# A graph-network kernel on one core: a block's table rows stored by one transfer of 125 rows in place of 112 and 13

## The chip, the core and the metric

The kernel runs on one core of one Trainium2 chip. The metric is device microseconds of one execution. Times and clocks of engines below are from the hardware profiler; PE is TensorE, DVE is VectorE, ACT is ScalarE, POOL is GpSimd, SP is SyncE.

## What is computed

`x` is 6250 nodes by 256 features, f32. After a layer norm it goes through three relational graph layers, a linear-attention mixer and a mixture of 8 experts. The change lies in the graph layers:

```python
def _rgcn_layer(x, W, root, bias, src, dst, seg):
    agg = jax.ops.segment_sum(x[src], seg, num_segments=N_REL * N_NODES)
    agg = agg.reshape(N_REL, N_NODES, -1)
    return jnp.einsum('rnd,rde->ne', agg, W) + x @ root + bias
...
for l in range(N_LAYERS - 1):
    h = jax.nn.relu(_rgcn_layer(h, weights[l], roots[l], biases[l], src, dst, seg))
h = jax.nn.sigmoid(_rgcn_layer(h, weights[-1], roots[-1], biases[-1], src, dst, seg))
```

There are 206,250 edges, sorted by `dst`, and 8 relations. Products and sums commute, so the kernel multiplies first: for each layer it makes a table in HBM that holds, for each node, its features times each of the 8 relation matrices (8 rows of 256 f32 a node, 8 KB), and then each edge fetches one 1 KB row of that table and adds it to its destination.

## The kernel before

Nodes are cut into NW = 50 blocks ("windows") of WIN = 125 nodes, one node a partition. Internally the stages are phase 0 (layer norm and the table of layer 1) and phases 1 to 3, one for each graph layer; in this text they are the first stage and layers 1, 2, 3. Each of layers 1 and 2 also makes the table of the next layer, block by block, behind its own sums, and layer 1 carries the mixer's projections, layer 2 its attention and MLP, layer 3 the experts.

POOL issues the gathers (L501): 1612 indirect transfers a layer, each of 128 edges (128 KB), into a ring of 8 chunks of 4 gathers in SBUF. Before a chunk it waits on `slots_free`, which PE raises; before a layer it waits (L486) until all stores of that layer's table have landed. SP turns landed gathers into `chunks_ready` (L428). DVE builds one-hot matrices (L994), and PE adds a block's gathered rows into PSUM with them (L1403). About 32 gathers fall to a block.

The table of the next layer: PE transposes the block's result (L1343), ACT copies it to `hT` (L564), PE multiplies it with the weights (`products`, L1371), and the results leave PSUM for `y_stage[parity]`, one of two buffers of 125 partitions: relation pairs 0, 2, 3 by ACT and pair 1 by DVE (`evac_y`, L517 and L835). Before it writes, `evac_y` waits on `table_stored[parity]`: the store of two blocks earlier has to have landed. Then `store_y` (L520) issues the block's stores from ACT's queue: 112 and then 13 partitions of 8 KB each, and in layers 1 and 2 a third, 125 partitions of 1 KB to `base`. Each transfer raises its semaphore by 16 in all. The last block of a stage or layer is stored by another function, `evac_and_store` (L533), in pieces of 4, 2 and 2 relations.

All transfers but SP's early loads and POOL's gathers go through ACT's queue, between ACT's own arithmetic and in program order. What is issued around the store:

- First stage, for each block: the table store of the block before, then the store of normalized rows to `xn_scratch` (L595, 125 x 1 KB), the load of `x` four blocks ahead (L597, 125 x 1 KB), the copy to `hT` (L564), and the next `evac_y`. Early in this stage SP loads the edge arrays, weights and vectors; among these `dst` twice for an order check (L384: 125 partitions of 6,600 B; L385: 124 of them).
- Layer 1: table store, `base` store, the load of the next block's `xn_in` (L627), then `xhat` (L630).
- Layer 2: table store (L527), `base` store (L530), `res_scratch` store (L740), loads of `base_in` (L619), `xn_in` (L699), `x_in` (L700), each 125 x 1 KB; only behind these seven issues stands the ACTIVATE of `xhatT` (L724) in ACT's program. PE needs `xhatT` for the MLP's up-projection (L1558), which stands between the third and fourth of the units of L1403 in PE's program (`phase2`).
- Layer 3 stores no table.

Of the kernel before, what the change touches and what calls it, by code (L numbers as in the profile page):

```python
# [26 lines left out]
WIN = 125  # L27
WIN_A = 112
# [8 lines left out]
def gps_program(nc, t):  # L37
    nodes, D = t["x"].shape
    edges = t["src"].shape[0]
    R = t["L0_gnn_weights"].shape[1]  # L40
    ROWS = R + 1
    K = D // 128
    NW = nodes // WIN
# [24 lines left out]
    table_nodes = [a.rearrange("(n r) d -> n (r d)", r=R) for a in table]  # L68
# [4 lines left out]
    with ExitStack() as ctx:  # L73
        ctx.enter_context(nc.allow_non_contiguous_dma(reason="a few vectors go to a feature a partition"))

        def sb(name, shape, dt=FP32):
            return ctx.enter_context(nc.sbuf_tensor(name, shape, dt))

        def sem(name):
            return ctx.enter_context(nc.semaphore(name))  # L80
# [18 lines left out]
        y_stage = [sb(f"y_stage{i}", [WIN, ROWS * D]) for i in range(2)]  # L99
# [146 lines left out]
        table_stored = [sem(f"table_stored{i}") for i in range(2)]  # L246
# [64 lines left out]

        def stored_before(phase, turn, parity=0):

            whole = 32 if phase == 0 else 48
            earlier = (32 + 48 * (phase - 1)) * (NW // 2) if phase else 0
            return earlier + turn * whole + (4 * 16 * phase if parity else 0)

        S_CHAIN, P2_CHAIN, P3_CHAIN, R_CHAIN = 3, 15, 13, 9

# [20 lines left out]
        def dve_blocks_before(phase, w):  # L340

            return w if phase == 0 else NW + ((phase - 1) * NW + w) * 2
# [94 lines left out]
        def _(pool):  # L437
# [45 lines left out]
            for l in range(3):  # L483

                for i in range(2):
                    pool.wait_ge(table_stored[i], stored_before(l + 1, 0, i))  # L486
                with pool.Fori(0, passes) as p:
                    before = pool.snap((passes * l + p) * CHUNKS)
                    for chunk in range(CHUNKS):
                        s = chunk % RING  # L490

                        if chunk >= CHUNKS - RING + LAST_CHUNKS:
                            continue
                        pool.wait_ge(slots_free, before + (chunk + 1))
                        apart(pool)
                        for j in range(TILES):
                            c = s * TILES + j
                            tile = chunk * TILES + j
                            n = min(TILE, edges - tile * TILE)
                            assert n > 0  # L500
                            nc.gpsimd.indirect_dma_start(  # L501
                                ring[0:n, c * D:(c + 1) * D], None, table[l],
                                bass.IndirectOffsetOnAxis(ap=gather_idx[0:n, tile:tile + 1].bitcast(U32), axis=0)
                                ).then_inc(gathered[s], 16)
# [3 lines left out]
        def _(act):  # L508
            def evac_y(phase, win, blocks):

                w, parity, turn = win
                T = w + phase * NW
                if 0 in blocks and not (phase == 0 and isinstance(w, int) and w < 2):
                    act.wait_ge(table_stored[parity], stored_before(phase, turn, parity))
                for b in blocks:
                    act.wait_ge(y_done, products_before(phase, w) + (ORDERS[phase].index(b) + 1))
                    nc.scalar.copy(y_stage[parity][:, b * 2 * D:(b + 1) * 2 * D],  # L517
                                   BANK[phase][b][0:WIN, 0:2 * D]).then_inc(y_evac_act, 1)

            def store_y(phase, win):  # L520

                w, parity, _ = win
                T = w + phase * NW
                act.wait_ge(y_evac_act, T * 3 + 3)
                act.wait_ge(y_evac_dve, dve_blocks_before(phase, w + 1))
                for p0, p1 in ((0, WIN_A), (WIN_A, WIN)):
                    act.dma_start(table_nodes[phase][bass.ds(w * WIN + p0, p1 - p0), :],  # L527
                                  y_stage[parity][p0:p1, 0:R * D]).then_inc(table_stored[parity], 16)
                if phase:
                    act.dma_start(rows(base_dram[phase - 1], w), y_stage[parity][:, R * D:ROWS * D]  # L530
                                  ).then_inc(table_stored[parity], 16)
# [35 lines left out]
            def rows(a, w):  # L567
                return a[bass.ds(w * WIN, WIN), :]
# [33 lines left out]
            def phase0_tail(win):  # L602
                evac_y(0, win, (0, 2, 3))
                store_y(0, win)
# [5 lines left out]
            for i in range(2):  # L610
                act.wait_ge(table_stored[i], stored_before(1, 0, i))
                act.wait_ge(xn_stored[i], 16 * (NW // 2))
# [8 lines left out]
            def phase1(cur, prev):  # L621
                w, parity, turn = cur
                if not (isinstance(w, int) and w == NW - 1):

                    if prev:
                        act.wait_ge(xhat_ready, w)
                    act.dma_start(xn_in[1 - parity][:, :], rows(xn_dram, w + 1)).then_inc(xn_loaded[1 - parity], 16)  # L627
                act.wait_ge(xn_loaded[parity], turn * 16 + 16)

                nc.scalar.activation(xhat[:, :], xn_in[parity][:, :], ACT.Identity,  # L630
                                     scale=ln1_scale[:, bass.ds(w, 1)],
                                     bias=ln1_shift[:, bass.ds(w, 1)]).then_inc(xhat_ready, 1)
                if prev:
                    copy_hT(1, prev, ACT.Relu)
                act.wait_ge(mixT_done, w + 1)
                for k in range(K):
                    last = nc.scalar.activation(xhatT[:, k, :], ps_a[:, k * WIN:(k + 1) * WIN], ACT.Identity,
                                                scale=cols[:, 0, k:k + 1], bias=cols[:, 1, k:k + 1])
                last.then_inc(xhatT_ready, 1)
                nc.scalar.copy(xnT[:, :, :], ps_a[:, K * WIN:2 * K * WIN].rearrange("p (k n) -> p k n", k=K)  # L640
                               ).then_inc(xnT_ready, 1)
                if prev:
                    evac_y(1, prev, (0,))
                if w < NW - 1:
                    projections(w)
                if prev:
                    evac_y(1, prev, (2, 3))
                    store_y(1, prev)
# [45 lines left out]
            def phase2(cur, prev):  # L694
                w, parity, turn = cur
                if w == 0:
                    warm(ACT.Gelu)
                load_base(1, w, parity)
                act.dma_start(xn_in[parity][:, :], rows(xn_dram, w)).then_inc(xn_loaded[parity], 16)  # L699
                act.dma_start(x_in[parity][:, :], rows(t["x"], w)).then_inc(x_loaded[parity], 16)  # L700
                if prev:
                    xhat_transposed(prev)
                    copy_hT(2, prev, ACT.Relu)
                    if w < NW - 1:
                        gelus(prev)
                    evac_y(2, prev, (0,))
                if w < NW - 1:
                    take_q(w)
                    copy_q(w + 1)
                if prev:  # L710
                    evac_y(2, prev, (2, 3))
                    store_y(2, prev)
                if prev and w < NW - 1:
                    store_res(prev)
# [1034 lines left out]
```

## Time and profile before

| | |
|---|---|
| runs | 7882.57 and 7892.93 us, median 7887.75 us |
| profiled execution, span from first to last instruction | 6522.0 us |
| profiled execution's own time | not given by the page; only the span is |
| mean granted TensorE clock | 0.920 |
| instructions | 82,564 |
| PE busy | 5410.7 us (83%) |
| POOL busy | 4625.3 us (71%) |
| DVE, ACT busy | 2019.4 us (31%), 1061.6 us (16%) |
| DMA | 887.88 MB in 354,380 packets |
| first gather starts | 389.1 us |
| last gather of layer 3 starts | 6487.9 us |

Busy time of POOL counts the gathers' own 947 ns; about 300 ns between two gathers are not counted. A share of "16 engines" is time that packets took, summed over the core's 16 DMA engines. The stages last from 20 to 389 us, 389 to 2404, 2424 to 4449 and 4471 to 6490; the gaps between layers are POOL's wait for the table.

### The profile page before, as it was taken

The page shows a single profiled execution, that of the slowest core. Times are in us where ns is not written, and L with a number is a line of the kernel's source. Part 1 is how long each engine was busy: PE and PEld are TensorE (multiplying, and loading weights), DVE is VectorE, ACT ScalarE, POOL GpSimd, SP SyncE. Part 2 cuts the span into 40 slices and gives each one's busy share as a digit, 9 for nine tenths or more (in the row PEclk, how much of TensorE's full clock was granted, in tenths as well). Part 3 has the DMA queues.
Part 4 walks back from the last instruction along what each step waited for, and adds up shares of the span by engine and source line. Part 5 has one row for each costly group of instructions (what it writes and reads, how often), then busy time and mean ns, then how long its engine had stood idle before and what let it go on. Part 6 is the DMA issues. An engine that isn't in the chain of part 4 may idle for free.

```text
span 6522.0 us, 82564 instructions
## 1 busy us (share of the span) xinstructions
PE 5410.7 (83%) x22990; PEld 4060.0 (62%) x22990; DVE 2019.4 (31%) x5385; ACT 1061.6 (16%) x2756; POOL 4625.3 (71%) x4909
## 2 busy tenths in 40 slices
PE   8977777777777778888888888887888888888888
PEld 4445555555555546666666666666777777777776
DVE  3321211122222223332333333333444444444444
ACT  2211111111111111111111111111222222222222
POOL 1057777777777767777777777776777777777776
PEclk9989898889898889999999999999999999999999
DMA  6654444444444444544554444444433333433333
GB/s 195 180 155 137 137 137 137 137 137 137 137 137 137 137 143 144 147 146 146 147 148 146 146 145 146 147 146 149 116 115 115 115 115 115 115 115 115 116 115 93
DMA packets 354380, 887.88 MB, mean 136 GB/s; under 512 B 86234, under 2 KB 179294, under 8 KB 335623
## 3 DMA queue, kind: packets, MB, share of 16 engines
q0 software_dynamic: 232080, 633.91, 33.0%
q10 hardware_dynamic: 114178, 243.16, 12.8%
q1 hardware_dynamic: 7740, 5.99, 0.3%
q8 instruction: 207, 3.39, 0.2%
q14 instruction: 175, 1.43, 0.1%
HBM read 697.11 MB, written 185.60 MB: 135 GB/s over the span
## 4 chain that ended last, share of the span: by engine, by line
POOL 44%; PE 30%; issue 15%; ACTq 5%; DMA 3%; ACT 1%; POOLq 1%; DVE 0%; DVEq 0%; SPq 0%
POOL ring L501 44%; PE ps_out L1403 11%; PE ps_y L1371 8%; PE ps_tr L1570 2%; PE ps_b L1558 2%; DMA ring<-table,gather_idx 2%; PE ps_c L1371 1%; PE ps_b L1371 1%; PE ps_c L1558 1%; ACTq L619 1%; ACTq L740 1%; ACTq L699 1%; ACT y_stage L517 1%; PE ps_y L1656 1%; ACTq L527 1%
## 5 line engine op out<-in xcount | busy, mean ns | idle before, releaser
L501 POOL DMA_INDIRECT ring<-table,gather_idx x4836 | 4580.7, 947 | 1519.4 <-issue 1487.8
L1403 PE MATMUL ps_out<-ring,onehot 128*125 x8400 | 2238.3, 419 | 709.7 <-SPq L428 671.1
L1403 PEld LDWEIGHTS ps_out<-ring,onehot 128*125 128x125 f32 x8400 | 1699.0, 209 | 1131.0 <-issue 857.7
L1371 PE MATMUL ps_y<-W,hT 128*125 128x512 f32 (+1 forms) x2400 | 1016.9, 564 | 0.9 <-ACT hT L564 0.9
L835 DVE COPY y_stage<-ps_y 125x512 f32<-125x512 f32 x150 | 103.7, 692 | 2425.6 <-PE ps_y L1371 2393.6
L1403 PE MATMUL ps_out<-ring,onehot_more 128*125 x2448 | 661.3, 421 | 131.9 <-SPq L428 87.4
L1371 PEld LDWEIGHTS ps_y<-W,hT 128*125 128x125 f32 x2400 | 455.8, 192 | 400.1 <-issue 372.7
L994 DVE TENSOR_TENSOR onehot<-targets,ps_out 128x500 f32<-128x500 f32 x1050 | 646.4, 671 | 172.1 <-issue 117.1
L1403 PEld LDWEIGHTS ps_out<-ring,onehot_more 128*125 128x125 f32 x2448 | 479.5, 205 | 286.8 <-issue 214.7
L517 ACT COPY y_stage<-ps_y 125x512 f32<-125x512 f32 x350 | 204.6, 585 | 1659.1 <-PE ps_y L1371 1653.8
L994 DVE TENSOR_TENSOR onehot_more<-targets,ps_out 128x250 f32<-128x250 f32 x612 | 240.9, 414 | 608.4 <-PE ps_out L1403 490.2
L1656 PE MATMUL ps_y<-hT,big 128*128 128x125 f32 x3200 | 417.0, 279 | 0.0
L1656 PEld LDWEIGHTS ps_y<-hT,big 128*128 128x128 f32 x3200 | 399.3, 193 | 27.7 <-issue 16.7
L796 ACT ACTIVATE gT<-ps_y,vectors 128x125 f32<-128x125 f32 x800 | 242.6, 363 | 473.9 <-PE ps_y L1656 473.2
L1558 PE MATMUL ps_b<-xhatT,big 128*128 128x125 f32 x800 | 167.0, 392 | 180.8 <-ACT xhatT L724 180.8
L564 ACT ACTIVATE hT<-ps_tr 128x250 f32<-128x250 f32 x200 | 75.9, 379 | 1334.0 <-PE ps_tr L1343 1169.8
L1558 PEld LDWEIGHTS ps_b<-xhatT,big 128*128 128x128 f32 x800 | 154.6, 297 | 200.4 <-ACT xhatT L724 200.0
L474 POOL TENSOR_TENSOR rstd<-mv,neg_half 125x1 f32<-125x1 f32 x50 | 33.0, 660 | 324.2 <-DVE mv L955 324.2
L1667 PE MATMUL ps_b<-big,gT 128*125 128x256 f32 x800 | 206.7, 381 | 1.0 <-ACT gT L796 1.0
L1667 PE MATMUL ps_c<-big,gT 128*125 128x256 f32 x800 | 197.4, 379 | 0.0
L1254 DVE SCALAR_TENSOR_TENSOR r<-ps_b,combine,r 125x256 f32<-125x256 f32 x200 | 96.8, 484 | 324.8 <-PE ps_b L1667 321.2
L1570 PE MATMUL ps_tr<-big,gT 128*125 128x256 f32 x800 | 180.9, 379 | 0.0
(193 smaller groups left out, 3208.2 us busy)
## 6 DMA issues: line engine op xcount, KB each, us to landing
table<-y_stage ACTq DMA_DIRECT2D x147, 896.0 KB
ring<-table,gather_idx POOLq DMA_INDIRECT x4836, 2.9
table<-y_stage ACTq DMA_DIRECT2D x147, 104.0 KB
xn_in<-xn_scratch ACTq DMA_DIRECT2D x100, 125.0 KB
base<-y_stage ACTq DMA_DIRECT2D x100, 125.0 KB
base_in<-base ACTq DMA_DIRECT2D x100, 125.0 KB
x_in<-in_x_dram ACTq DMA_DIRECT2D x75, 125.0 KB
xn_scratch<-xn_in ACTq DMA_DIRECT2D x50, 125.0 KB
```

Of the source, the lines that this page charges most:

```text
L501: nc.gpsimd.indirect_dma_start(ring[0:n, c * D:(c + 1) * D], None, table[l], bass.IndirectOffsetOnAxis(ap=gather_idx[0:n, tile:tile + 1].b ...
L517: nc.scalar.copy(y_stage[parity][:, b * 2 * D:(b + 1) * 2 * D], BANK[phase][b][0:WIN, 0:2 * D]).then_inc(y_evac_act, 1)
L796: last = nc.scalar.activation(gT[:, (e % GB) * K + f, :], ps_y[e % 2][:, f * WIN:(f + 1) * WIN], ACT.Gelu, bias=b1e[:, e, f:f + 1])
L835: nc.vector.tensor_copy(y_stage[parity][:, 2 * D:4 * D], BANK[phase][1][0:WIN, 0:2 * D]).then_inc(y_evac_dve, 1)
L994: return nc.vector.tensor_tensor(out, targets[:, bass.ds(col, count)].unsqueeze(2).broadcast_to([128, count, n]), nodes.unsqueeze(1).broad ...
L1254: nc.vector.scalar_tensor_tensor(out=acc[parity][:, :], in0=(ps_b, ps_c)[e // 2 % 2][0:WIN, e % 2 * D:(e % 2 + 1) * D], scalar=combine[:, ...
L1371: last = nc.tensor.matmul(BANK[phase][b][0:WIN, 0:n], hT[parity][:, k, :], W[:, k, b * 2 * D:b * 2 * D + n], start=(k == 0), stop=(k == K ...
L1403: return nc.tensor.matmul(ps_out[w % 2][0:WIN, 0:D], lhsT, ring[:, bass.ds(slot + j * D, D)], start=first, stop=last)
L1558: last = nc.tensor.matmul(bank[:, (j % 4) * WIN:(j % 4 + 1) * WIN], W1[:, k, j * 128:(j + 1) * 128], xhatT[:, k, :], start=(k == 0), stop= ...
L1570: last = nc.tensor.matmul(ps_tr[0:WIN, D:2 * D], gT[:, j, :], W2[:, j, :], start=(j == 0), stop=(j == FJ - 1))
L1656: last = nc.tensor.matmul(ps_y[e % 2][:, f * WIN:(f + 1) * WIN], w1e[:, e, k, f * 128:(f + 1) * 128], hT[parity][:, k, :], start=(k == 0), ...
L1667: last = nc.tensor.matmul((ps_b, ps_c)[e // 2 % 2][0:WIN, e % 2 * D:(e % 2 + 1) * D], gT[:, (e % GB) * K + f, :], w2e[:, e, f, :], start=( ...
```

## The change

For every block but a layer's last, the two transfers of 112 and 13 partitions become one of 125. The bytes, the buffers and the order of everything else stay. The counts on `table_stored` are lowered to match: a block raises it by 16 in place of 32 in the first stage, and by 32 in place of 48 in layers 1 and 2; the correction for the odd parity, in which the last block lies, is now five transfers a stage (six pieces of the last block in place of one).

```diff
         def stored_before(phase, turn, parity=0):
 
-            whole = 32 if phase == 0 else 48
-            earlier = (32 + 48 * (phase - 1)) * (NW // 2) if phase else 0
-            return earlier + turn * whole + (4 * 16 * phase if parity else 0)
+            whole = 16 if phase == 0 else 32
+            earlier = (16 + 32 * (phase - 1)) * (NW // 2) if phase else 0
+            return earlier + turn * whole + (5 * 16 * phase if parity else 0)
...
-                for p0, p1 in ((0, WIN_A), (WIN_A, WIN)):
-                    act.dma_start(table_nodes[phase][bass.ds(w * WIN + p0, p1 - p0), :],
-                                  y_stage[parity][p0:p1, 0:R * D]).then_inc(table_stored[parity], 16)
+                act.dma_start(table_nodes[phase][bass.ds(w * WIN, WIN), :],
+                              y_stage[parity][:, 0:R * D]).then_inc(table_stored[parity], 16)
```

## Rows read from the trace of the kernel before

**Rows 1.** the page: span, busy time, share of the chain that ended last

```profile
span 6522.0 us, 82564 instructions
...
PE 5410.7 (83%) x22990; PEld 4060.0 (62%) x22990; DVE 2019.4 (31%) x5385; ACT 1061.6 (16%) x2756; POOL 4625.3 (71%) x4909
...
POOL 44%; PE 30%; issue 15%; ACTq 5%; DMA 3%; ACT 1%; POOLq 1%; DVE 0%; DVEq 0%; SPq 0%
```

**Rows 2.** busy time of each engine by stage: first stage, layer 1, layer 2

```profile
core 0: us, PE busy (x) PEld busy (x) DVE busy (x) ACT busy (x) POOL busy (x), PEclk, DMA share, GB/s
20.00:388.00 368.00, 355.13 (x911) 158.59 (x909) 122.83 (x386) 100.04 (x196) 38.13 (x47) 0.98 0.62 184
389.00:2404.00 2015.00, 1519.35 (x5663) 1096.97 (x5664) 399.82 (x800) 234.89 (x541) 1524.13 (x1612) 0.89 0.47 137
2424.00:4449.00 2025.00, 1752.81 (x7325) 1326.92 (x7326) 624.17 (x1645) 263.46 (x779) 1530.36 (x1612) 0.92 0.50 147
```

**Rows 3.** longest waits of PE and its releaser, layer 1 (us, times, longest)

```profile
PE ps_out L1403 <- SPq L428: 497.0, 199, 14.3
```

**Rows 4.** the same in layer 2

```profile
PE ps_b L1558 <- ACT xhatT L724: 178.9, 47, 5.8
```

**Rows 5.** the gathers on POOL, layer 1 and then layer 2

```profile
L501 POOL DMA_INDIRECT ring<-table,gather_idx x1612 | 1524.3, 946 | 491.2 <-issue 488.5 <-PE ps_out L1403 2.7
...
L501 POOL DMA_INDIRECT ring<-table,gather_idx x1612 | 1531.0, 950 | 514.4 <-issue 496.8 <-PE ps_out L1403 17.6
```

**Rows 6.** the chain that ended last, one block of layer 2 (start, us, what)

```profile
3533.57 0.59 ACT y_stage L517
...
3534.18 0.32 ACTq L527
...
3537.74 1.78 ACTq L619
...
3541.48 0.81 ACT xhatT L724 x2
...
3542.34 2.44 PE ps_b L1558 x16
```

**Rows 7.** ACT's queue in the first stage: the first store and two later ones

```profile
20.09 0.77 ACTq L527 DMA_DIRECT2D table<-y_stage  x2
...
307.43 0.76 ACTq L527 DMA_DIRECT2D table<-y_stage  x2
...
314.52 0.76 ACTq L527 DMA_DIRECT2D table<-y_stage  x2
```

**Rows 8.** DMA over ten blocks of the first stage (queue: packets, MB, share)

```profile
DMA packets 3872, 12.57 MB, mean 177 GB/s; under 512 B 380, under 2 KB 2619, under 8 KB 2619
...
q10 hardware_dynamic: 3869, 12.53, 60.0%
```

**Rows 9.** DMA, 314.3 to 315.2 us

```profile
q10 hardware_dynamic: 85, 0.08, 26.1%
```

**Rows 10.** DMA, 32 to 44 us: SP's reads of dst (queue: packets, MB, share)

```profile
q1 hardware_dynamic: 207, 1.06, 21.9%
```

**Rows 11.** ACT in the first stage, behind those reads

```profile
36.64 7.97 ACTq L597 DMA_DIRECT2D x_in<-in_x_dram  x1
44.66 0.38 ACT L564 ACTIVATE hT<-ps_tr 128x250 f32<-128x250 f32 x1 [10.42 <-issue]
```

**Rows 12.** DMA of layer 2, store's issue to last load's, 3534.18 to 3541.44

```profile
q10 hardware_dynamic: 220, 1.09, 52.0%
q0 software_dynamic: 199, 0.53, 26.3%
```

**Rows 13.** DMA over the whole of layer 2

```profile
q0 software_dynamic: 77280, 211.13, 34.9%
```

**Rows 14.** between layers 1 and 2: the last whole store, and POOL

```profile
2409.09 0.76 ACTq L527 DMA_DIRECT2D table<-y_stage  x2
...
2423.93 0.98 POOL L501 DMA_INDIRECT ring<-table,gather_idx  x1 [19.77 <-issue]
```

## The prediction

> **What bounds the kernel now.** I read the page first: a span of 6522.0 us, PE busy 83%, and a chain of waits that is 44% gathers on POOL, 30% PE and, a small but telling share, 5% ACT's queue [rows 1]. An average over stages says little, so next the windows by stage: first stage 368 us with PE busy 355, layer 1 with PE busy 1519 of 2015, layer 2 with 1753 of 2025 [rows 2]. Then each stage's waits. The first stage is PE's: 7.09 us a block, from one store to the next (314.52 - 307.43) [rows 7]. In layer 1 PE waits 497 us for gathers [rows 3], and POOL issues one each (1524.3 + 491.2) / 1612 = 1.250 us and hardly waits [rows 5]: POOL is the bound, with some 10 us of slack a block on PE's side (497/49). Layer 2 looks alike (1.257 us a gather) but is not: PE no longer waits for gathers; it waits for ACT's `xhatT`, 178.9 us in 47 blocks, 3.8 us each [rows 4]. The chain of one block shows why: last copy to `y_stage`, then seven DMA issues from 3534.18, then `xhatT` at 3541.48, then PE [rows 6]. So 7.3 us of each of layer 2's 40.3 us are ACT issuing, and a microsecond more there is a microsecond more in the loop.
>
> **How 125 rows are carried.** Ten blocks of the first stage have 380 packets under 512 B, 38 a block [rows 8]. Taken as one completion packet for each DMA engine at work, 112 rows give 16, 13 rows give 13, and the two 125-row transfers of 1 KB (one of the two ends with block 45) must share the remaining 9: five each, not 16. A stretch that holds only 1 KB packets of such transfers confirms it: 26.1% of 16 engines, 4.2 engines [rows 9]. I take five: 25 rows of 8 KB an engine for the new store, 204.8 KB, in place of 7 or 8 rows (at most 65.5 KB).
>
> The Trainium skill (DMA: Bandwidth & Descriptors, section "Why a DMA increments its semaphore by 16 and not by 1") has a rule that speaks against this change: a transfer runs on the largest number of engines, up to 16, that divides its row count. By it 112 gives 16, 13 gives 13 and 125 gives 5; the trace agrees (38 small packets, 4.2 engines), and without the rule the sum would stand on those rows alone.
>
> **Speed of one engine.** The nearest row is SP's reading of `dst` in rows of 6,600 B, itself a transfer of 125 and one of 124 partitions: 1.06 MB in 21.9% of 16 engines over 12 us, 42.0 engine-us, 25.2 GB/s [rows 10]. The other bound is the first stage with all 16 engines crowded at each store: 12.53 MB in 60.0% x 16 x 70.85 us, 18.4 GB/s [rows 8]. Five engines don't crowd, so I take 25.2: the store then needs 8.1 us (bound 11.1), a 1 KB transfer of 125 rows 1.0 us (1.4).
>
> **First stage.** Removed: 49 issues of about 0.4 us on ACT (half of 0.76 [rows 7]), which lie beside PE's work: nothing. Added: each of the five engines carries 8.1 + 1.0 + 1.0 = 10.1 us a block, where PE takes 7.09. The stage becomes bound by those five. Store w must land before `evac_y` of w + 2; until then the queue holds store w + 1 and the small transfers, so it doesn't run dry. From the first store (issued at 20.1 [rows 7], moving at about 22): 49 stores x 8.1 = 398, 49 stores of `xn_scratch` 50, 45 loads 46, the last block's pieces 3, and SP's `dst` reads on the same engines, 25 + 31 rows x 6,600 B = 370 KB, 15 us. Sum 512, so the last store lands near 536 instead of 388 [rows 2]: **+147 us**. Ends: 9.6 us a block (if 8 KB rows go 5% better than 6.6 KB ones) gives +125, 18.4 GB/s gives +330, which I weigh little since it comes from crowding.
>
> **Layer 1.** One engine of the five has 8.1 + 2.0 us of ACT's transfers and its gather share within 40.3 us. ACT's queue behind the store holds `base` and one load (75 rows an engine), fewer than the 108 that layer 2 queues today before its last load. What is later, `xn_in` of the next block, is due 40 us on; gathers may land a microsecond late, covered by the ring and PE's 10 us. 0 us; if that cover were gone, 1 us x 49.
>
> **Layer 2.** The removed issue saves 0.4 us of ACT, if ACT's issues stay free. They don't when engines are backed up: behind SP's slow reads one issue took 7.97 us, and ACT's next ACTIVATE started at 44.66 [rows 11]. How much may be outstanding? When today's x_in issue ends (3541.44), 8 + 5 x 25 = 133 rows an engine have been handed over; moved are 1.09 MB, that is 1.02 of table rows and about 64 rows of 1 KB, 13 on each of five [rows 12]. 133 - 8 - 13 = 112 outstanding. After the change 150 are handed over, so if 112 is about what fits, x_in's issue ends when 38 have moved: all 25 table rows (8.1 us) and 13 small ones (0.5 us), 8.6 engine-us. Gathers share those engines, 34.9% of their time over the layer and 26.3% in that window [rows 12, 13], both with crowding; I take 25%: 11.5 us, plus 1.3 us until the first row moves (estimated from the gap between issue and traffic), 12.8 in place of 7.3. **5.5 us a block on the loop, x 47 = +258 us.** Ends: no sharing 9.9 us, +2.6, +122; 35% 14.5 us, +7.2, +338; and if all 150 rows fit, -0.4 us x 47 = -19, cut to -10 because POOL's own pace is 1.250 against 1.257 us (0.0063 x 1612 [rows 5]). What is late next: PE at the up-projection, then POOL, whose slots PE frees. `xn_in` and `x_in` land some 7 us later, in a block of 40; their readers stand near its end.
>
> **Between layers.** The last whole store is issued at 2409.09, POOL restarts at 2423.93 [rows 14]. The five engines then have 8.1 + 1.0 + 2.6 + 1.0 us of work from 2411, done at 2423.7; landed 1 us later than now. Two layers, +2 us.
>
> **Sum.** +147 + 258 + 2 = +407 us: the span goes to 6929. The median of the runs is 7887.75, 1366 us above the span, which the page doesn't explain; I add the same 407 to it: **8295 us**, 5% up. A change under 2% (158 us) is what a measurement can't tell from none.
>
> **The rivals.** (A) The forecast, 0.67: 7888 + 147 + 122 or 338 + 2 gives 8159 to 8375. (B) Only the first stage pays, because 150 rows fit in the queue, or because the 1366 us are spent inside the layers in unprofiled runs (0.28 us a gather, 9 us a block, would cover 5.5): 7888 + 147 - 0 to 10 = 8030 to 8037. For it: no issue in layer 2 is seen truly stuck. Against: [rows 11], and a chain through ACT's issues. 0.20. (C) Not slower: the 125 rows spread over as many engines as now; then there are 147 fewer issues, and only layer 2's loop feels it, -10 us: 7878. It decides from 8 engines on: 8.1 x 5 / 8 = 5.1 us of table rows and 2.0 of small ones fit the first stage's 7.09, and layer 2's queue has 16 rows more than 125, near today's 8. Against it stand 38 small packets and 4.2 engines. 0.05. The Trainium skill (same page, section "Rules for kernel authors") advises one 128-partition transfer over two disjoint halves; by that the change would gain as in C, yet its rule is for 128 rows. (D) Five loaded engines also hold up gathers, so that PE falls behind in both layers, 1 us a block on 98 blocks above A: 8390. Against: PE's slack in layer 1. 0.08.
>
> **How the numbers follow.** The likeliest is A, 8295. From B's bottom, 8030, to D, 8430, leaves out C and the tail of D. Slower by over 2% means above 8045: A, D and a quarter of B, 0.80. Within 2%: the rest of B and C, 0.18. Faster by 2% has no mechanism: 0.02.
>
> **What would show it.** First gather near 536, not 389; one store each 10.1 us in the first stage, with DMA at a steady 5/16 and about 130 GB/s; DVE and ACT waiting on `table_stored` there. Layer 1's span unchanged. In layer 2 issues of L699 and L700 of several microseconds, PE's wait for `xhatT` near 9 us, POOL waiting on PE. Wrong would be: short issues in layer 2 (then B), or over five engines at work (C).

## The result, and the profile after

The changed kernel takes **8171.09 us** (8162.49 to 8179.68) against 7887.75 us: 283 us more, a ratio of 1.0357, 95% interval 1.0326 to 1.0389. The forecast was 8295, in a range of 8030 to 8430.

The page of after is of an execution of 8177.9 us, close to the timed runs. That of before, at 6522.0 us [rows 1], was far faster than every timed run. So the kernel before was profiled once more, at 7992.8 us, on a chip where it is timed at 8014 to 8027 us (medians), and the layers are compared with that trace. First the page of after; "another core or an unknown queue", in other views "remote", is what the profile could not name.

```profile
span 8177.9 us, 82417 instructions
...
PE 5664.2 (69%) x22990; PEld 4226.9 (52%) x22990; DVE 2018.1 (25%) x5385; ACT 1052.0 (13%) x2756; POOL 4634.9 (57%) x4909
...
PE 38%; another core or an unknown queue 28%; issue 14%; DMA 5%; DVE 5%; ACTq 4%; ACT 4%; DVEq 1%; POOL 0%; POOLq 0%; SPq 0%
```

Next busy time by stage (from, to, length; busy time of each engine; granted clock of PE; DMA share; GB/s): after, in the first stage and the three layers,

```profile
core 0: us, PE busy (x) PEld busy (x) DVE busy (x) ACT busy (x) POOL busy (x), PEclk, DMA share, GB/s
20.00:532.00 512.00, 390.67 (x910) 166.85 (x908) 123.90 (x392) 96.50 (x195) 39.05 (x47) 0.92 0.34 134
533.00:2915.00 2382.00, 1504.22 (x5637) 1098.50 (x5638) 391.62 (x788) 228.30 (x540) 1527.34 (x1612) 0.79 0.38 115
2944.00:5515.00 2571.00, 1842.67 (x7297) 1377.72 (x7298) 624.03 (x1640) 261.67 (x775) 1530.18 (x1612) 0.83 0.38 115
5550.00:8124.00 2574.00, 1816.07 (x8667) 1507.91 (x8666) 838.72 (x2448) 433.17 (x1165) 1529.27 (x1612) 0.84 0.32 92
```

and the same stages of the kernel before, profiled again.

```profile
20.00:390.00 370.00, 355.52 (x909) 158.93 (x907) 123.02 (x387) 99.47 (x195) 38.73 (x47) 0.98 0.62 183
390.00:2790.00 2400.00, 1485.85 (x5635) 1085.65 (x5636) 393.54 (x794) 225.39 (x540) 1523.25 (x1612) 0.80 0.39 115
2819.00:5286.00 2467.00, 1879.94 (x7291) 1356.94 (x7292) 626.64 (x1640) 259.13 (x775) 1526.57 (x1612) 0.86 0.41 120
5318.00:7936.00 2618.00, 1796.33 (x8674) 1491.90 (x8672) 836.39 (x2442) 432.75 (x1166) 1526.26 (x1612) 0.83 0.31 90
```

Against [rows 2], PE's work is nearly the same in the first stage, 355.5 us of 370, but layer 1 takes 2400 us in place of 2014, layer 2 2467 in place of 2025 and layer 3 2618 in place of 2017. That is 1429 of the 1471 us between the two profiles of before, so the 1366 us that I could not place very likely lie inside the layers too. After, the first stage lasts 143 us longer, layer 1 is 17 us shorter (2 in a second trace of after, below), and layer 2 is 103 us longer here and 146 in the second trace. Layer 3, which the change does not touch, is 43 us shorter here and 9 longer in the second trace. So a layer of the first trace of after, from another round, compares with this one only to some 40 us; the second is from the same round and chip. In the first stage DMA fell from 62% to 34% of 16 engines with about the same bytes to move.

**First stage after.** ACT's queue around two stores (start, length, what):

```profile
405.80 0.26 ACTq L526 DMA_DIRECT2D table<-y_stage  x1
406.09 4.62 ACTq L594 DMA_DIRECT2D xn_scratch<-xn_in  x1
...
414.85 0.26 ACTq L526 DMA_DIRECT2D table<-y_stage  x1
```

One store to the next is 9.05 us here; [rows 7] had 7.09. Over the stage it is (532.7 - 389.1) / 49 = 2.93 us more, 10.0 in all. The issue of `xn_scratch` now sticks for 4.62 us behind the store. DVE's wait for the store of two blocks earlier (us, times, longest; in the first profile of before 32.0 us in 6 waits), and DMA over ten blocks (queue: packets, MB, share of 16 engines):

```profile
DVE y_stage L834 <- DMA table<-y_stage: 334.8, 45, 19.8
```

```profile
DMA packets 3850, 13.12 MB, mean 130 GB/s; under 512 B 149, under 2 KB 2549, under 8 KB 2549
...
q10 hardware_dynamic: 3848, 13.10, 32.0%
```

There are 149 packets under 512 B, 15 a block: three transfers of five each, where [rows 8] had 38. The queue's share, 32.0% of 16, is 5.1 engines. While it is busy, one engine moves 13.10 MB / (0.320 x 16 x 101 us) = 25.3 GB/s.

**Layer 2 after.** ACT's queue in one block, from the table store's issue to `xhatT`, to be held against the chain of [rows 6]:

```profile
5049.40 0.26 ACTq L526 DMA_DIRECT2D table<-y_stage  x1
...
5051.96 7.16 ACTq L698 DMA_DIRECT2D xn_in<-xn_scratch  x1
5059.15 1.13 ACTq L699 DMA_DIRECT2D x_in<-in_x_dram  x1
5060.33 0.80 ACT L723 ACTIVATE xhatT<-ps_a,vectors 128x125 f32<-128x125 f32 x2 [10.96 <-issue]
```

and DMA in that stretch.

```profile
q10 hardware_dynamic: 123, 1.01, 27.1%
```

Where the kernel before issued seven transfers in 7.3 us, six now take 10.9, and one of them, `xn_in`, holds ACT for 7.16. The queue moved 123 packets, 1.01 MB: all 8 KB rows, none of 1 KB. Up to the end of `xn_in`'s issue (5049.40 to 5059.12) it had begun 114 of them:

```profile
q10 hardware_dynamic: 114, 0.93, 27.6%
```

**Between layers** POOL's gap grew from 28.7 to 29.3 us (layers 1 and 2) and from 31.9 to 34.8 us (2 and 3).

### The profile page after: what moved, and what is told of

Same layout as the page of the kernel before. It is cut to its first block, busy times and chain, and to the rows that moved or that the text cites. A ratio compares the mean times of both kernels' runs of the same rounds, so it can differ in the third digit from the quotient of the medians.

```text
span 8177.9 us, 82417 instructions
## 1 busy us (share of the span) xinstructions
PE 5664.2 (69%) x22990; PEld 4226.9 (52%) x22990; DVE 2018.1 (25%) x5385; ACT 1052.0 (13%) x2756; POOL 4634.9 (57%) x4909
## 4 chain that ended last, share of the span: by engine, by line
PE 38%; another core or an unknown queue 28%; issue 14%; DMA 5%; DVE 5%; ACTq 4%; ACT 4%; DVEq 1%; POOL 0%; POOLq 0%; SPq 0%
PE ps_out L1402 17%; PE ps_y L1370 5%; DMA table<-y_stage 5%; PE ps_y L1655 4%; ACTq L698 3%; PE ps_b L1557 2%; PE ps_b L1666 2%; PE ps_tr L1569 2%; PE ps_c L1666 1%; PE ps_c L1557 1%; DVE onehot L993 1%; DVE r L1253 1%; ACT y_stage L517 1%; DVEq L325 1%
## 5 line engine op out<-in xcount | busy, mean ns | idle before, releaser
L501 POOL DMA_INDIRECT ring<-table,gather_idx x4836 | 4590.0, 949 | 3006.5 <-issue 1407.7
L1402 PE MATMUL ps_out<-ring,onehot 128*125 x8400 | 2079.3, 398 | 119.6 <-issue 49.4
L1402 PEld LDWEIGHTS ps_out<-ring,onehot 128*125 128x125 f32 x8400 | 1618.8, 198 | 456.6 <-issue 210.7
L1402 PE MATMUL ps_out<-ring,onehot_more 128*125 x2448 | 821.5, 495 | 818.6 <-DVE onehot_more L993 600.8
L1402 PEld LDWEIGHTS ps_out<-ring,onehot_more 128*125 128x125 f32 x2448 | 575.4, 247 | 1044.7 <-issue 937.2
L1370 PE MATMUL ps_y<-W,hT 128*125 128x512 f32 (+1 forms) x2400 | 1064.3, 584 | 53.9 <-issue 23.5
L1655 PE MATMUL ps_y<-hT,big 128*128 128x125 f32 x3200 | 490.7, 307 | 166.2 <-ACT gT L795 145.9
L1655 PEld LDWEIGHTS ps_y<-hT,big 128*128 128x128 f32 x3200 | 467.9, 220 | 207.4 <-ACT gT L795 152.4
L1342 PE MATMUL ps_tr<-ident,xhat 125*128 125x125 f32 x100 | 33.0, 430 | 394.8 <-DVE xhat L1209 295.0
L1666 PE MATMUL ps_b<-big,gT 128*125 128x256 f32 x800 | 242.9, 432 | 82.2 <-ACT gT L795 65.8
L1612 PE MATMUL ps_a<-kvWo,qT 32*125 32x256 f32 x100 | 55.9, 655 | 294.3 <-ACT qT L718 212.9
```

What stands on the lines that cost most here:

```text
L501: nc.gpsimd.indirect_dma_start(ring[0:n, c * D:(c + 1) * D], None, table[l], bass.IndirectOffsetOnAxis(ap=gather_idx[0:n, tile:tile + 1].b ...
L1370: last = nc.tensor.matmul(BANK[phase][b][0:WIN, 0:n], hT[parity][:, k, :], W[:, k, b * 2 * D:b * 2 * D + n], start=(k == 0), stop=(k == K ...
L1402: return nc.tensor.matmul(ps_out[w % 2][0:WIN, 0:D], lhsT, ring[:, bass.ds(slot + j * D, D)], start=first, stop=last)
L1655: last = nc.tensor.matmul(ps_y[e % 2][:, f * WIN:(f + 1) * WIN], w1e[:, e, k, f * 128:(f + 1) * 128], hT[parity][:, k, :], start=(k == 0), ...
L1666: last = nc.tensor.matmul((ps_b, ps_c)[e // 2 % 2][0:WIN, e % 2 * D:(e % 2 + 1) * D], gT[:, (e % GB) * K + f, :], w2e[:, e, f, :], start=( ...
```

## The experiments

The theory was the forecast's: the store runs on five engines, so that the first stage becomes bound by those five, and in layer 2 ACT's issues stick behind it, which holds up `xhatT`. Against it stood that the layers' extra time covers the delay (B), that loaded engines hold up gathers (D), and that the transfer spreads (C). Kernels of one round share a chip; every ratio is to the kernel before on that chip. Traces are less comparable: of the kernel before there is one for the chip of experiments 1 and 2 only. Layer 2 with its transfers and their order as before lasted 2467.4 and 2475.4 us there, 2504.7 on the chip of experiments 3 and 4 (the kernel with 124 rows) and 2454.8 on that of 5 to 7 (the kernel of 6). "First gather" is the start of the first L501, the end of the first stage's path.

**1. Both kernels again.**

```diff
 (no edit: the kernel before; the kernel after)
```

> The kernel before, unchanged, for a profile taken beside its timed runs: the profile that I predicted from had a span of 6522 us while the runs took 7888, and the changed kernel's profile has a span within 2 us of its own time. If the 1366 us lie inside the span (the loops run slower in these runs), this profile shows a span of about 7886, a first stage that still ends near 389 us, and layers of about 2380 to 2570 us in place of 2015 to 2025. If they lie outside it, the span is again 6522.

> The changed kernel again beside the others on one chip: 1.036 times the kernel before, about +283 us. By my theory, the first stage ends at 533 us (+144) and layer 2 is some 139 us longer, with 7 us stuck issues of the load of xn_in in ACT's queue. By the rival that the five loaded engines delay gathers, layer 1 is longer too.

Ratios 0.9986 [0.9970, 1.0001] and 1.0333 [1.0302, 1.0363]. First gathers, before and then after:

```profile
390.18 1.22 POOL L501 DMA_INDIRECT ring<-table,gather_idx  x1 [0.45 <-issue]
```

```profile
534.09 1.22 POOL L501 DMA_INDIRECT ring<-table,gather_idx  x1 [3.83 <-issue]
```

144 us in the first stage, and in layer 2 2613.1 against 2467.4 us: 146. Layer 1 is 2397.9 against 2399.6 us. The two differences sum to 290 of the 304 us between the two spans.

**2. One part at a time.** The new store in the first stage alone, and in layer 2 alone:

```diff
-for p0, p1 in ((0, WIN_A), (WIN_A, WIN)):
+for p0, p1 in (((0, WIN),) if phase in (0,) else ((0, WIN_A), (WIN_A, WIN))):   # or (2,)
```

> 125 rows in one transfer in the first stage only, 112 and 13 in layers 1 and 2. My theory: first gather at 533 us, +144 us over the kernel before, and nothing in the layers: ratio 1.018. The rival that the first stage's delay is taken back later, since POOL or PE wait less: under +50 us, ratio under 1.006.

> 125 rows in one transfer in layer 2 only. My theory (ACT's queue is stuck behind the slow store, and PE waits for xhatT): +120 to +260 us, with issues of the load of xn_in of 7 us in place of 1.3, and the other stages unchanged; by what the changed kernel's total leaves over for it, +139, ratio 1.018. The rival (only the first stage pays, the layers' own pace hides it): within 20 us of the kernel before. The rival that gathers are delayed in both layers: about half of 139 here, the other half in layer 1.

Ratios 1.0155 [1.0126, 1.0184] and 1.0171 [1.0143, 1.0199]; their excesses sum to 3.26%, the whole change has 3.33%. So the two add up, and nothing clear of the intervals is left for layer 1. With the first stage alone the first gather starts at 529.77 us, 140 us late; the ratio, a little under the expected 1.018, gives 124 (101 to 148).

With layer 2 alone, layer 2 lasts 2617.3 us, 149.9 more, and the median from store issue to `xhatT` over 47 blocks goes from 7.33 to 11.02 us. PE's waits in layer 2 (us, times, longest), before and then with the edit (its lines lie three further down):

```profile
PE ps_b L1558 <- issue: 84.8, 26, 4.6
PE ps_b L1558 <- ACT xhatT L724: 77.2, 21, 9.0
...
PE ps_a L1613 <- ACT qT L719: 58.3, 21, 8.6
```

```profile
PE ps_a L1616 <- ACT qT L722: 258.3, 41, 9.0
PE ps_b L1561 <- issue: 186.2, 25, 9.4
PE ps_b L1561 <- ACT xhatT L727: 151.9, 22, 8.5
```

At the up-projection PE idles 186.2 + 151.9 = 338 us in place of 162, 176 more. That is 47 x 3.7, the whole delay, as the theory has it. (In about half of the blocks the list has it under "issue", time in which the engine waited for nothing that the profile shows.) At `qT` it idles longer too, by 200 us on the line shown. Yet the layer grew by 150 only: the other waits in the two lists, shorter by 204 us, absorbed the rest, and PE was busy 25 us less. POOL's waits show who pays, before and then with the edit:

```profile
POOL ring L501 <- issue: 481.6, 1392, 27.8
POOL ring L501 <- remote: 276.3, 90, 4.7
POOL ring L501 <- PE ps_out L1403: 210.3, 130, 18.3
```

```profile
POOL ring L504 <- issue: 483.2, 1399, 28.1
POOL ring L504 <- PE ps_out L1406: 477.6, 142, 17.1
POOL ring L504 <- remote: 159.0, 71, 5.0
```

POOL waits 968 us before and 1120 after, 152 more, which is the layer's growth; its wait for PE to free slots went from 210 to 478 us, and the one that the profile could not name ("remote") fell by 117.

**3. Other row counts.** 124 rows and 1 in the first stage; and 100 and 25 everywhere.

```diff
-for p0, p1 in ((0, WIN_A), (WIN_A, WIN)):
+cut = WIN_A if phase else 124
+for p0, p1 in ((0, cut), (cut, WIN)):
```

```diff
-for p0, p1 in ((0, WIN_A), (WIN_A, WIN)):
+for p0, p1 in ((0, 100), (100, WIN)):
```

> First stage only: 124 and 1 rows in place of 112 and 13; still two transfers, the layers as before. My theory (the engines share out rows by a divisor of the row count, here 4, and the busiest engine sets the stage): 31 rows of 8 KB at 0.31 to 0.32 us and 2.0 us of small rows are 11.6 to 12.0 us a block, first gather at 610 to 630 us in place of 390, +220 to +240 us, ratio 1.028. The rival that it is the single large transfer, not the number of engines, that is slow: two transfers, no change.

> 100 and 25 rows in all stages. By divisors, 10 engines with 10 rows and 5 with 5: at most 15 rows an engine, 4.7 us, plus 2.0 us of small rows, under the first stage's 7.09. My theory: first gather within 10 us of 390; in layer 2 no stuck issue or one under 2 us, +0 to +60 us; ratio 1.000 to 1.008. The rival that any uneven split costs the first stage: first gather after 430 us.

Ratios 1.0304 [1.0264, 1.0345] and 1.0201 [1.0166, 1.0236]. First gathers:

```profile
639.27 1.22 POOL L501 DMA_INDIRECT ring<-table,gather_idx  x1 [8.49 <-issue]
```

```profile
422.57 1.22 POOL L501 DMA_INDIRECT ring<-table,gather_idx  x1 [2.08 <-issue]
```

The 124 rows cost 249 us, more than 125: what counts is not how many rows but how many engines they fall on. With 31 rows of 8 KB on each of four engines, at 0.31 us (the median time of such a packet), and the two small transfers at the forecast's 1.0 us each, a block is estimated at 31 x 0.31 + 2.0 = 11.6 us, near the measured 7.09 + 249 / 49 = 12.2. The Trainium skill (DMA: Bandwidth & Descriptors, section "Why a DMA increments its semaphore by 16 and not by 1") states that the engines are the largest number up to 16 that divides the row count, so 4 for 124; this run's trace agrees (from 300 to 422 us, ten blocks, 145 packets under 512 B, and 26.7% of 16 engines, 4.3), and for 125 the trace of after agrees in 15 small packets a block and 5.1 engines.

100 and 25 was my miss. I had the first gather within 10 us of before and found 32 more, and layer 2 at most 60 us longer and found 134 (2601.3), or 97 against the 2504.7 us of the same chip; the timed runs leave 129 us for all that is behind the first stage (0.0201 x 8034.5 - 32). By the count that fits 124 and 125, the 100 rows lie on ten engines and the 25 on five, at most 15 rows of 8 KB on one, where 112 and 13 make 8. ACT's issues stick even then, in layer 2 this one load for 3.61 us:

```profile
4093.89 3.61 ACTq L699 DMA_DIRECT2D xn_in<-xn_scratch  x1
...
4099.19 0.80 ACT L724 ACTIVATE xhatT<-ps_a,vectors 128x125 f32<-128x125 f32 x2 [9.77 <-issue]
```

The median from store issue to `xhatT` was 9.97 us. In the first stage 15 rows and the small transfers make 15 x 0.31 + 2.0 = 6.6 us, less than PE's 7.09, and yet a block took 7.09 + 32 / 49 = 7.75. The DMA from 300 to 371 us, 9.2 such blocks, shows why the count alone falls short:

```profile
DMA packets 3690, 11.89 MB, mean 167 GB/s; under 512 B 232, under 2 KB 2527, under 8 KB 2527
...
q10 hardware_dynamic: 3689, 11.87, 49.8%
```

There are 25 small packets a block, as ten, five, five and five engines would give. But one busy engine moves only 11.87 MB / (0.498 x 16 x 71 us) = 21.0 GB/s, between the 25.3 with five engines at work and the 18.4 with all 16 [rows 8]. The fullest engine's 15 rows of 8 KB and 50 of 1 KB, 174 KB, need 6.9 us at 25.3 GB/s and 8.3 us at 21.0, and the measured 7.75 lies between. So a row costs more where more engines are at work, and the median of 0.31 us hides it. This is an estimate; no run tried it.

**4. Where in the order.** The new store in layer 2 alone, but issued behind `xhatT`; and, with 112 and 13 rows kept, all of layer 2's issues behind `xhatT`:

```diff
 xhat_transposed(prev)
+if w >= 2:
+    store_y(2, window(w - 2))
...
-store_y(2, ...)          # at the iteration's end, now only if w == NW - 1
```

```diff
+xhat_transposed(prev)
+store_y(2, window(w - 2)); store_res(window(w - 2))
 ...                      # then the three loads, as before
-xhat_transposed(prev)
```

> As layer2_only, 125 rows in one transfer in layer 2, but a block's table and base stores are issued one iteration later, behind the ACTIVATE of xhatT. My theory (the loss is ACT's stuck queue in front of xhatT): layer 2's loss of 150 us goes, no issue of 7 us stands before xhatT, and with two issues fewer there it is 0 to 100 us under the kernel before: ratio 0.987 to 1.000. The rival that the five loaded engines delay gathers or loads of the block: the store takes as long as it did, so +150 us stays, ratio 1.017.

> The kernel before with 112 and 13 rows, and in layer 2 all of a block's transfers (table, base, res, and the three loads) issued behind the ACTIVATE of xhatT. If the 7.3 us of issues are on layer 2's path, PE's wait for xhatT (about 4 us a block) goes: -100 to -190 us, ratio 0.976 to 0.988. If another wait takes its place (hT and the gelus come behind the same issues now): within 30 us of the kernel before.

Ratios 0.9966 [0.9952, 0.9981] and 0.9958 [0.9942, 0.9975]. The same 125-row transfers that cost 137 us in experiment 2 cost nothing here: the runs are 27 us shorter than before. Layer 2 lasts 2455.0 us, 50 less than the 2504.7 of the same chip. With 112 and 13 rows and all issues behind `xhatT`, the runs are 34 us shorter and layer 2 lasts 2462.9 us; that is about its expectation's second branch, within 30 us, and not the gain of 100 to 190 us. With the new store behind `xhatT`, ACT issues the loads at once, then `xhatT`, then the store:

```profile
4042.85 0.39 ACTq L702 DMA_DIRECT2D xn_in<-xn_scratch  x1
4043.27 0.42 ACTq L703 DMA_DIRECT2D x_in<-in_x_dram  x1
4044.10 0.46 ACT L730 ACTIVATE xhatT<-ps_a,vectors 128x125 f32<-128x125 f32 x1 [1.36 <-PE ps_a L1552]
4044.16 0.26 ACTq L530 DMA_DIRECT2D table<-y_stage  x1
```

This refutes D in layer 2: the five engines carry the same rows beside the same gathers. Both kernels also show how little the wait for `xhatT` was worth in these executions. In the first of them it is gone from PE's list, and others stand there:

```profile
PE ps_out L1409 <- issue: 184.4, 197, 6.9
PE ps_y L1377 <- issue: 100.0, 82, 5.5
PE ps_y L1377 <- DVE y_stage L844: 82.8, 20, 6.9
```

**5. The delay alone.** No transfer is changed; 24 or 12 small copies on ACT stand ahead of `xhatT` in layer 2.

```diff
+for i in range(24):      # or 12
+    nc.scalar.copy(spare[:, i * 32:(i + 1) * 32], ident[:, 0:32])
 xhat_transposed(prev)
```

> The kernel before, with 112 and 13 rows, and 24 small copies added on ACT in layer 2, between the last load's issue and the ACTIVATE of xhatT: about 3.7 us a block, as long as the changed kernel's stuck issue adds (3.65), and no change to any transfer. My theory (only the time at which xhatT comes counts): layer 2 is 140 to 180 us longer, ratio 1.017 to 1.022. The rival (the loss is in the five loaded engines: late gathers, late base_in or x_in): under 60 us.

> The same with 12 copies, 1.8 to 1.9 us a block. If the loss is in proportion to the delay: +75 to +90 us, ratio 1.010. If it comes as a step once PE's wait grows beyond some point, as 100 and 25 rows suggest (about 2 us later, layer 2 +134): +120 to +150 us, nearly that of the long delay, and a mean granted clock nearer 0.83 than 0.86 in layer 2.

Ratios 1.0147 [1.0118, 1.0175] and 1.0039 [1.0026, 1.0052]: 116 us for 3.0 us of delay (median 10.31 against 7.33), 31 us for 1.7 (9.02). The long one gives 116 / 3.0 = 39 us for each microsecond, the new store in layer 2 alone 137 / 3.7 = 37. So ACT's delay by itself explains that part. The short one gives only 18, so the price does not look linear, and part of the first microsecond or two finds cover; both branches of its expectation, +75 to +90 and +120 to +150, were too high. The traces show the bend more weakly: layer 2 lasts 2566.7 and 2502.7 us, 112 and 48 more than the 2454.8 of the same chip, or 38 and 28 us a microsecond.

**6. The small store in the first stage.** As the first-stage edit, with `xn_scratch`'s 125 rows stored as 112 and 13:

```diff
-act.dma_start(rows(xn_dram, w), xn_in[parity][:, :]).then_inc(xn_stored[parity], 16)
+for p0, p1 in ((0, WIN_A), (WIN_A, WIN)):
+    act.dma_start(xn_dram[w * WIN + p0:w * WIN + p1, :],
+                  xn_in[parity][p0:p1, :]).then_inc(xn_stored[parity], 16)
...                      # the waits on xn_stored are raised to match
```

> As first_stage_only, 125 rows in one transfer in the first stage, but the 1 KB rows of xn_scratch are stored as 112 and 13 rows, so that the five engines carry at most 8 of them in place of 25. My theory (the first stage runs at the sum of work on the busiest engine): 0.7 us a block less, first gather at about 497 us in place of 530 to 534; ratio 1.011 to 1.012. The rival (the table store's own time from issue to landing sets the block, whatever else the engines carry): first gather still at 530 to 534.

Ratio 1.0137 [1.0115, 1.0158]. First gather:

```profile
495.66 1.22 POOL L504 DMA_INDIRECT ring<-table,gather_idx  x1 [2.61 <-issue]
```

That is 34 us earlier than in experiment 2, 0.7 us a block: 1.0 us of 1 KB rows (an estimate, 25.6 KB at 25.3 GB/s) left each of the five engines and 0.3 came back. So what the five engines have queued paces the first stage, and not the table store's own time.

**7. The better version.** 112 and 13 rows in the first stage, 125 in layers 1 and 2, and layer 2's table and `base` stores behind `xhatT` (the edits of 2, for phases 1 and 2, and 4):

> A version to keep: 112 and 13 rows in the first stage, 125 rows in one transfer in layers 1 and 2, and in layer 2 the table and base stores behind the ACTIVATE of xhatT. My theory (only the first stage's engines and ACT's stuck queue in layer 2 make one large store on five engines dear): layer 1 as before, layer 2 about 12 us shorter, ratio 0.995 to 0.999. The rival (one store on five engines costs something in every layer): ratio above 1.002.

Ratio 0.9975 [0.9961, 0.9989], 7862.39 us against 7883.18. It beats both kernels, by a quarter of a per cent over before. Layer 2 takes 2422.0 us, against 2454.8 in the kernel of experiment 6, whose layers are as before, on the same chip; layer 1 gives 14 us of that back (2380.1 against 2366.3, where the two kernels of experiment 5 had 2364.3 and 2365.6), so a 125-row store in layer 1 may not be quite free, though the chip of experiment 2 did not show it. Since the second kernel of experiment 4 gains as much without any 125-row store, this points to the order and not the transfer as what gains.

## Why the prediction was right, and where it was off

**First stage, right.** Predicted +147 us, a first gather near 536 and five engines at 25.2 GB/s; measured +143.6 (532.7), 15 completion packets a block and 25.3 GB/s. The predicted 10.1 us a block was 10.0. Experiments 2, 6 and the 124 rows of 3 move the number as a count of rows on engines says; 100 and 25 rows do so only with a slower engine.

**Layer 1, right.** Predicted 0; -17 and -2 us in two traces of after, and the parts sum without it. Only experiment 7 has it 14 us longer.

**Between layers, nearly right.** Predicted +2 us together; 0.6 + 2.9 in one trace, 2.0 + 2.8 in the other.

**Layer 2: the mechanism right, the term mis-sized.** Predicted 5.5 us x 47 = 258; measured 3.7 us of delay and 137 to 150 us. Most of the distance from 8295 to 8171 is this term. Two things were off.

The failed step is "if 112 is about what fits, x_in's issue ends when 38 have moved". The rows of layer 2 after show 123 table rows begun, 24.6 an engine, and no small one when that issue ended: 150 handed over less 25 is 125 outstanding. I had worked out 112 from a stretch in which the queue need not have been full, which makes it a lower bound, and I used it as the limit. With 25 rows in place of 38, and the first row moving after 0.8 us in place of 1.3, the stretch is 10.9 us, not 12.8. What stuck was mostly `xn_in`'s issue, 7.16 us, where `x_in`'s took 1.13. A fixed limit on outstanding rows does not explain that either. When `xn_in`'s issue ended, 125 rows an engine had been handed over and 23 begun, 102 outstanding; `x_in`'s then went through within 1.13 us, up to 125. By what rule an issue is held stays open.

The other is the factor 47, "a microsecond more there is a microsecond more in the loop". A microsecond of delay in ACT's path cost 37 to 41 us over the layer. In the trace that I read, PE waited for `xhatT` in all 47 blocks [rows 4]; profiled again, near the times of the timed runs, the list names it in 21, and other waits of PE shrank by 204 us when this one grew. So part of the delay was covered.

Two sums of the prediction are slightly off and change nothing: layer 2's block is 2025 / 50 = 40.5 us and not 40.3, and B's 7888 + 147 + 2, less 0 to 10, is 8027 to 8037.

**The rivals.** B had its premise right, as the missing time lies inside the layers, and its conclusion wrong: 14 to 21% of the 174 us (47 x 3.7) was covered, not all of it. C is refuted by 15 small packets a block; D by experiment 4 in layer 2 and by layer 1's unchanged length in after.

## What to carry to other kernels

Count a store by the rows that its busiest engine gets, not by its number of transfers, and allow for slower rows when many engines are at work (18.4 to 25.3 GB/s an engine here). In this kernel one transfer fewer a block cost 143 us in 49 blocks where its 8 KB rows paced the stage. If such a transfer must stay, issue it behind whatever the issuing engine still owes others, because issues that follow it can be held until rows have moved. And profile the kernel at the speed at which it is timed before multiplying a wait by its count.

## What the runs showed of the hardware beyond that

An issue on ACT is not free when one engine's queue is long: the same load took 0.39 us with the store behind it and 7.16 us with the store ahead.

What lies between 6522 and 7993 us of the same kernel is not settled. PE's granted clock in layer 2 was 0.92 in [rows 2] and 0.86 when profiled again, and with the new store in layer 2 it falls further:

```profile
2815.00:5433.00 2618.00, 1855.34 (x7297) 1376.59 (x7298) 625.08 (x1640) 261.06 (x775) 1525.82 (x1612) 0.83 0.37 113
```

Two levels, 1.2 and 2.4 GHz, make 0.86 a share of (1 - 0.86) x 2 = 28% at the low one, 691 of 2467 us, and 0.83 makes 34%, 890 of 2618 us. PE was granted the low level for longer where it idled more; how much of the 150 us that explains was not tried. The clock may not be all of it: in places the readers of products also start late. In the trace of after eight products start at the usual pace, and their two readers follow 4.92 us apart:

```profile
5020.45 3.60 PE L1370 MATMUL ps_y<-W,hT 128*125 128x512 f32 x8
...
5026.01 0.69 DVE L834 COPY y_stage<-ps_y 125x512 f32<-125x512 f32 x1 [27.23 <-remote]
...
5030.93 0.59 ACT L517 COPY y_stage<-ps_y 125x512 f32<-125x512 f32 x1 [12.42 <-remote]
```

In the first profile of before it was 1.71 us:

```profile
3553.20 3.60 PE L1371 MATMUL ps_y<-W,hT 128*125 128x512 f32 x8
...
3555.18 0.69 DVE L835 COPY y_stage<-ps_y 125x512 f32<-125x512 f32 x1 [21.63 <-PE ps_y L1371]
...
3556.89 0.58 ACT L517 COPY y_stage<-ps_y 125x512 f32<-125x512 f32 x1 [5.93 <-PE ps_y L1371]
```

The granted clock around the late one was

```profile
5020.00:5031.00 11.00, 4.05 (x11) 1.69 (x9) 1.43 (x3) 0.07 (x1) 6.64 (x7) 0.86 0.33 95
```

a low level for 28% of those 11 us, some 3.1 us. Even if all of it lay between the two readers, it could add at most half of that, 1.5 us, and 1.71 would become 3.3, not 4.92. The cause stays open.
